# Where the low parts of the attention weights are made, and in which order every engine works: a fused attention and feed-forward kernel

## What is computed

```python
def _L0_attn_ref(x, W_qkv, W_out):
    qkv = x @ W_qkv.T
    q, k, v = jnp.split(qkv, 3, axis=-1)
    ...
    q = phi(q); k = phi(k)                      # elu(x) + 1
    kv_cumsum = jnp.cumsum(k * v, axis=2)
    k_cumsum = jnp.cumsum(k, axis=2)
    out = q * kv_cumsum / (q * k_cumsum + EPS)
    return out @ W_out.T * HD ** (-0.5)

def _L0_ffn_ref(x, w_gate_up, w_proj):
    gu = jnp.einsum('bsd,hd->bsh', x, ternary_quant(w_gate_up))
    gate, up = jnp.split(gu, 2, axis=-1)
    hn = rms_norm(jax.nn.silu(gate) * up)
    return jnp.einsum('bsh,dh->bsd', hn, ternary_quant(w_proj))

x = x + _layernorm(_L0_attn_ref(_layernorm(x), W_qkv, W_out))
x = x + _layernorm(_L0_ffn_ref(_layernorm(x), w_gate_up, w_proj))
```

## Time and profile before

| | |
|---|---|
| runs | 1148.55, 1148.72, 1149.49 us |
| profiled execution | 1149.28 us, of which the span from first to last instruction is 1147.3 us |
| TensorE busy | 1055.8 us, 92% |
| VectorE busy | 805.6 us, 70% |
| GpSimd busy | 561.5 us, 49% |
| ScalarE busy | 487.8 us, 43% |
| mean granted TensorE clock | 0.983 of full |

### The profile page before, as it was taken

The page is one execution under the profiler, slowest core; times in us unless marked ns, Lnnn a source line. Parts: engine busy times, 40 slices in busy tenths (PEclk is TensorE's granted clock), DMA queues, the critical chain, the costliest instruction groups (busy, mean ns, idle before and its releaser), DMA issues.

```text
span 1147.3 us, 14246 instructions
## 1 busy us (share of the span) xinstructions
PE 1055.8 (92%) x5041; PEld 521.7 (45%) x5088; DVE 805.6 (70%) x1233; ACT 487.8 (43%) x808; POOL 561.5 (49%) x494
## 2 busy tenths in 40 slices
PE   3887778988999999999999999999999999999997
PEld 1434344444544454446444454446444454454443
DVE  5899999998557868645884568645884569845424
ACT  4543647664643214542364324542364325423433
POOL 4977548788543534523535234523535244534323
PEclk9998799999999999999999999999999999999999
DMA  7631234410022123003300123003300121001001
GB/s 238 143 97 46 65 101 111 157 56 19 1 74 74 37 74 74 1 8 63 91 24 1 29 83 74 1 10 63 95 18 1 29 83 37 7 32 37 1 1 73
DMA packets 105142, 63.83 MB, mean 56 GB/s; under 512 B 77424, under 2 KB 85616, under 8 KB 105072
## 3 DMA queue, kind: packets, MB, share of 16 engines
q1 hardware_dynamic: 105072, 62.93, 21.1%
HBM read 34.60 MB, written 9.44 MB: 38 GB/s over the span
## 4 chain that ended last, share of the span: by engine, by line
PE 56%; DVE 21%; POOL 6%; issue 6%; ACT 3%; DMA 0%; DVEq 0%; POOLq 0%; ACTq 0%; SPq 0%
PE bank L658 27%; PE bank L693 15%; PE bank L647 6%; PE bank L781 6%; DVE tk L1675 2%; POOL xn L1352 2%; DVE ts L1647 1%; DVE st L1585 1%; DVE grs L1504 1%; DVE hid L1727 1%; DVE x L1771 1%; DVE yq L1540 1%; DVE yq L1554 1%; DVE tr L1657 1%; DVE tq L1621 1%
## 5 line engine op out<-in xcount | busy, mean ns | idle before, releaser
L658 PE MATMUL bank<-x3t,wgu_t 128*128 128x512 f16 x1536 | 347.7, 381 | 15.1 <-DMA x3t<-x3s 8.5
L1363 POOL TENSOR_TENSOR acc<-acc,ht 128x512 f32<-128x512 f32 x90 | 118.3, 1315 | 295.7 <-ACT ht L1055 293.6
L658 PEld LDWEIGHTS bank<-x3t,wgu_t 128*128 128x128 bf16 x1536 | 148.6, 98 | 197.2 <-issue 13.5
L693 PE MATMUL bank<-wproj_t,hid 128*128 128x512 bf16 x830 | 192.8, 379 | 2.7 <-DVE tr L1637 0.5
L1721 DVE TENSOR_TENSOR ht<-ht,bank 128x512 f32<-128x512 f32 x112 | 76.4, 682 | 162.2 <-ACT ht L1016 83.2
L647 PE MATMUL bank<-xnt,wqkv_hi 128*128 128x512 f16 x672 | 163.5, 387 | 13.4 <-issue 10.7
L693 PEld LDWEIGHTS bank<-wproj_t,hid 128*128 128x128 f16 x872 | 84.8, 98 | 101.3 <-DVE tr L1637 1.0
L1727 DVE TENSOR_TENSOR hid<-ht,hid 128x512 f16<-128x512 f32 x109 | 89.5, 821 | 35.1 <-ACT hid L1043 34.0
L1016 ACT ACTIVATE ht<-bank 128x512 f32<-128x512 f32 x112 | 66.4, 593 | 111.2 <-PE bank L658 58.2
L1043 ACT ACTIVATE hid<-ht 128x512 f16<-128x512 f32 x109 | 68.2, 626 | 106.5 <-DVE ht L1721 105.1
L647 PEld LDWEIGHTS bank<-xnt,wqkv_hi 128*128 128x128 f16 x672 | 65.8, 100 | 96.4 <-issue 19.8
(11 more groups left out here) (187 smaller groups left out, 1622.8 us busy)
## 6 DMA issues: line engine op xcount, KB each, us to landing
raw_q<-in_L_ffn_w_gate_up_dram SPq DMA_DIRECT2D x32, 256.0 KB, 2.9
out_dram<-xn SPq DMA_DIRECT2D x7, 1024.0 KB, 8.4
...
```

What stands on the lines that cost most here:

```text
L658: last = pe.matmul(bank[:], wgu_t[:, k, first_row:first_row + P], x3t_of(f)[:, part, k], start=(n == 0), stop=(n == 2 * KD - 1))
L693: last = pe.matmul(bank[:], hid_of(f, part, k)[:, t * P:(t + 1) * P], wproj_t[:, k], start=(k == 0 and part == 0), stop=(k == MT - 1 and p ...
L1363: pool.tensor_tensor(acc[:], acc[:], ht_of(f)[:, m % 2], ALU.add).then_inc(q["acc_done"], 1)
```

## The change

Three things are done. The low parts of tiles 2 and 3 are made on VectorE like those of tiles 0 and 1: `weight_lo` of GpSimd is gone, that of VectorE takes the wait for the buffer, and one semaphore counts all twelve. The lists of all five engines are written anew, in `start()`, `step(s)` and `last_steps()`. No other instruction is added, left out or changed.

```diff
         def wait_low_weights(eng, j, part):
 
-            if j < 2:
-                eng.wait_ge(w_lo, 3 * j + part + 1)
-            else:
-                eng.wait_ge(w_lo_b, 3 * (j - 2) + part + 1)
+            eng.wait_ge(w_lo, 3 * j + part + 1)
...
-            def weight_lo(j, *parts):
-
-                for part in parts:
-                    pool.wait_ge(w_enlarge, powers_for(j))
-                    pool.wait_ge(w_hi, 3 * j + part + 1)
-                    if part == 0:
-                        wait_turned_weights(pool, j - 2)
-                    own_instruction(pool)
-                    pool.tensor_scalar(raw_a[j][:, part], raw_a[j][:, part], enlarge[:, j, part:part + 1], None, ALU.mult).then_inc(w_scaled, 1)
-                    pool.wait_ge(w_scaled, 3 * (j - 2) + part + 1)
-                    pool.tensor_tensor(wsplit[j % 2][:, 1, part], raw_a[j][:, part], wsplit[j % 2][:, 0, part], ALU.subtract).then_inc(w_lo_b, 1)
...
                 for part in parts:
                     dve.wait_ge(w_enlarge, powers_for(j))
                     dve.wait_ge(w_hi, 3 * j + part + 1)
+                    if j >= 2 and part == 0:
+                        wait_turned_weights(dve, j - 2)
                     dve.scalar_tensor_tensor(wsplit[j % 2][:, 1, part], raw_a[j][:, part], enlarge[:, j, part:part + 1],
                                              wsplit[j % 2][:, 0, part], ALU.mult, ALU.subtract).then_inc(w_lo, 1)
```

Of SyncE's list in `start()`, the lines that hold the transposes of the weights:

```diff
-                turn_high_weights(2), load_half(2), turn_x(1, 0, 1), turn_low_weights(2), load_half(0)
-                turn_high_weights(3), turn_x(1, 2, 3), turn_low_weights(3), load_half(3, 4, 5, 7), load_residual(0)
+                turn_high_weights(1), load_raw(4), turn_high_weights(2), turn_x(1, 0), turn_low_weights(2)
+                turn_x(1, 1, 2), load_half(1, 2), turn_high_weights(3), turn_low_weights(3), turn_x(1, 3)
```

More of the change, by code:

```diff
@@ L843, in step @@
+                gate_unit(1, 12), up_unit(1, 12), gate_unit(1, 13), up_unit(1, 13, 14), gate_unit(1, 14, 15)
+                up_unit(1, 15), group(2, 0, 1, 2, 3, 4), square_sums(1), group(2, 5, 6), project(1, 0, 1, 2, 3, 4)
+                group(2, 7), project(1, 5), group(2, 8, 9, 10), project(1, 6), group(2, 11)
+                project(1, 7, 8, 9, 10, 11, 12, 13, 14, 15), group(3, 0, 1), project_att(2, 0, 1, 2, 3), group(3, 2)
             def step(s):
                 f = s - 1
[L845 removed]
@@ new lines, in start @@
+                stats_var("3", 0), sum_keys(1, 2), back_reciprocal(1, 1), carry_key(1, 2), front_products(1, 2)
+                back_output(1, 1), x3_lo(0, 0), scale_sums(5), back_lo(1, 1), x3_lo(0, 1), scale_max(5), clip(2, 3)
+                diff(1), x3_lo(0, 2), feature_q(1, 3), scale_rec(5), x3_lo(0, 3), sum_values(1, 2), round_off(2)
+                feature_k(1, 3), carry_value(1, 2), scale_sums(6), front_products(1, 3), row_shrink(1), diff(2)
+                round_off(3), clip(4), back_reciprocal(1, 2), scale_row(4), scale_max(6), sum_keys(1, 3), diff(3)
@@ new lines, in start @@
+                scale_sums(7), sum_values(1, 3), scale_row(5), carry_key(1, 3), hidden_value(0, 0), scale_bound(2)
+                scale_rec(6), carry_value(1, 3), round_off(4), back_reciprocal(1, 3), back_output(1, 2)
+                hidden_value(0, 1), scale_max(7), back_output(1, 3), back_lo(1, 2), diff(4), back_lo(1, 3)
+                scale_sums(8), clip(5, 6), round_off(5), hidden_lo(0, 0), stats_tile("2", 1, 0), scale_max(8)
+                scale_rec(7), round_off(6), scale_row(6), hidden_lo(0, 1), scale_sums(9), scale_rec(8)
@@ new lines, in start @@
+                hidden_value(0, 2), scale_max(9), diff(5), stats_tile("2", 1, 1, 2), row_shrink(2), hidden_lo(0, 2)
+                stats_tile("2", 1, 3), stats_join("2", 1, 0, 1, 2, 3), scale_row(7), stats_mean("2", 1)
+                stats_var("2", 1), clip(7), diff(6), scale_rec(9), scale_bound(3), clip(8), hidden_value(0, 3)
+                add_ln2_tile(1, 0, 1, 2), stats_tile("3", 1, 0), add_ln2_tile(1, 3), round_off(7), stats_tile("3", 1, 1)
+                scale_sums(10), stats_tile("3", 1, 2), hidden_lo(0, 3), round_off(8), diff(7), stats_tile("3", 1, 3)
@@ new lines, in start @@
+                hidden_value(0, 6), round_off(11), diff(10), scale_max(14), hidden_lo(0, 6), row_shrink(4)
+                scale_rec(13), scale_row(10), scale_sums(15), hidden_value(1, 0), clip(12), scale_rec(14), scale_max(15)
+                diff(11), scale_rec(15), round_off(12), scale_row(11), clip(13), hidden_lo(1, 0), scale_sums(16)
+                scale_bound(5), diff(12), hidden_value(0, 7), round_off(13), scale_sums(17), hidden_lo(0, 7)
+                scale_max(16), hidden_value(1, 1), scale_max(17), clip(14), hidden_value(0, 8), hidden_lo(1, 1)
@@ new lines, in start @@
+                scale_rec(16), diff(13), clip(15), round_off(14), hidden_lo(0, 8), round_off(15), scale_row(12)
+                scale_sums(18), clip(16), diff(14), row_shrink(5), scale_max(18), scale_row(13), scale_rec(17)
+                hidden_value(1, 2), hidden_value(0, 9), scale_bound(6), round_off(16), diff(15), clip(17)
+                hidden_lo(1, 2), stats_tile("1", 2, 0), hidden_value(1, 3), stats_tile("1", 2, 1), scale_rec(18)
+                round_off(17), hidden_lo(0, 9), diff(16), scale_sums(19), hidden_lo(1, 3), row_shrink(6), clip(18)
@@ new lines, in start @@
+                scale_max(19), scale_rec(19), hidden_value(0, 10), scale_sums(20), hidden_lo(0, 10), diff(17)
+                scale_max(20), round_off(18), stats_tile("1", 2, 2), hidden_value(1, 4), scale_sums(21), scale_max(21)
+                scale_rec(20), clip(19), hidden_value(0, 11), clip(20), round_off(19), scale_row(14), diff(18)
+                hidden_lo(1, 4), scale_rec(21), hidden_value(1, 5), diff(19), scale_sums(22), round_off(20)
+                scale_row(15), hidden_value(0, 12), scale_sums(23), scale_max(22), hidden_lo(1, 5), scale_bound(7)
@@ new lines, in start @@
+                diff(20), stats_tile("1", 2, 3), scale_max(23), clip(21), hidden_lo(0, 11), stats_join("1", 2, 0)
+                hidden_lo(0, 12), stats_join("1", 2, 1), scale_rec(22), stats_join("1", 2, 2), row_shrink(7)
+                hidden_value(1, 6), hidden_value(0, 13), scale_rec(23), hidden_lo(1, 6), round_off(21)
+                stats_join("1", 2, 3), hidden_lo(0, 13), stats_mean("1", 2), clip(22), round_off(22), diff(21)
+                hidden_value(1, 7), stats_var("1", 2), clip(23), hidden_value(0, 14), round_off(23), hidden_value(1, 8)
```

646 lines of the change are left out of this document (305 added, 341 removed).

## The result

The changed kernel takes 1118.5 us (median of 4 runs, 1116.7 to 1120.1) against 1149.1 us of the one before in the same session: a ratio of 0.973, 95% interval 0.971 to 0.975. The profiled execution has a span of 1116.2 us against 1147.3 us.

What follows compares the result with a forecast made beforehand. VectorE was taken to bound the start (to 287 us) and TensorE the rest. From 1149.3 us, -5 for the start and -7 for the steps gave 1137.3, less 0.6 to the median: 1136.7 us; range 1127 to 1149.

Steps and rivals of the forecast that it cites:

- one seventh of the 37 us: Start, 29 to 287 us: the new lists save VectorE 5 us of the turns it loses beside GpSimd.
- the four groups: Start: VectorE's diff (9.0 us), clip (13.1), round_off (7.9) and hidden_lo (7.2), whose time above their lone values makes 37 us.
- The start's best case: Second rival: the start gains 16 us, the whole kernel taking 1125.7 us; chance 0.14.
- 7.3 us of waits: Start: TensorE's two early waits for low parts of tiles 2 and 3, 3.59 and 3.69 us, can go.
- The low parts as a draw: Start: on VectorE, 4.4 us of added low-part work against 4 us of turns given back; taken as 0.
- The first rival: The start gains nothing, low parts and their lost turns eating what GpSimd's absence gives: 1141.7 us; chance 0.20.
- The steps: Steady steps: 10 us of TensorE's waits go and 3 us of a new wait come, -7 us in all.
- The 2.8 us of waits for the bank: Steady steps: TensorE's three waits for ScalarE's exp to read the features from a bank, 2.8 us, go.
- The wait at square_sums: Steady steps: a new TensorE wait for GpSimd's squares behind the projection, 0.8 us in each of four steps, 3 us.
- The tail: End of the kernel: the chain of statistics, power and addition per tile is kept; taken as 0.
- The middle: From 287 to 430 us, where TensorE idles 5.4 us: no clear sign, taken as 0 with 2 us either way.
- The third rival: Steps: reciprocal before the last hidden tile comes 3.1 us later than reckoned, steps +5.6 us, 1154.3 us; chance 0.16.

Runs made afterwards that it cites:

- e1: The kernel before with only the low parts of tiles 2 and 3 made on VectorE, other lists as before: 1148.0 us, ratio 0.9985.
- e4: The changed kernel with only the low parts of tiles 2 and 3 put back on GpSimd: 1126.3 us, ratio 0.980.
- e10: The kernel before with GpSimd's divide and scale_back each replaced by three one-input scalings as 128x512 float32, ternary weights not computed rightly: 1221.7 us.
- e3: The changed kernel with last_steps() of all engines as in the kernel before: 1115.3 us, ratio 0.970.

## Why the prediction was wrong

**The step that failed** is "I take one seventh of the 37 us, 5 us, near the low end": the start gave 28.9 us. The mechanism, turns that VectorE loses beside GpSimd's two-input work, was the right one; its size was not, and both factors were too small. The 37 us came from the four groups of the earlier trace rows alone; over all of VectorE's instructions that take turns it is 66.2 us. The features, the running sums, the low parts of x, x3 and the output, and the hidden parts written to hid_b and hid_early (6.0 us) were left out. The features, sums and low parts had more to give than the four kinds: features 8.7 us, sums 6.3, low parts 5.7, against which the low weights and one product lost 3.4 more; 17.3 us net. Diff, clip, round_off and the hidden parts, all three buffers of them, lost 13.9 us less. And the share that can be avoided was 31 of 66 us, nearly half. The reason given, "there are hardly more free places on VectorE than before", counted the reciprocals alone. Reductions, statistics and what reads PSUM take no turns here either: before, 24 reductions took 1.15 to 1.22 us each, 20 statistics 0.63 to 0.69 and 24 `hidden_value` 0.63 to 0.69, whatever GpSimd did. GpSimd's large two-input operations, 165 us to 287 us before and 150 us to 257 us after, lay beside VectorE instructions that take turns for 100 us before and 63 us after, beside reciprocals for 14 and 20, beside the others for 54 and 71.

**The start's best case**, 16 us, had the same fault: "7.3 us of waits and a quarter of the 37". The result lies 13 us beyond it.

**The low parts as a draw** was right by itself: -1.5 us (e1). Its cost was low, since six low parts took 1.08 us in the mean and not 0.73. What it missed is that the move gains value with the lists, 7.8 us (e4): "VectorE bounds the stretch, so this only lets it start earlier" no longer holds once VectorE's turns are gone: without the move it was idle 12.1 us from 40 to 60 us.

**The rule of exclusion.** The first rival rested on the Trainium skill (SBUF — State Buffer, section "Who interferes with whom"), by which a two-input instruction of VectorE contends with any GpSimd instruction that reads SBUF, the port pair that they share being an exclusive lock. For two-input work of GpSimd the rows bear it out: 1.1 us lost in the mean beside scale_back and beside divide. Beside one-input work they do not: in e10, where the scalings lasted 1.49 us, 93 instructions of VectorE that met no other large operation lost 0.15 us in the mean and 0.43 at most. The rival did not come.

**The steps** came out at -6.1 for -7, by other terms. The waits that end from step 4 to step 7 are 7.2 us for x3t before and 3.2 us after, 4.0 us less where 7.2 were reckoned; nearly all that is left, 2.3 us, is the one at step 7, ahead of which the new list has one group less. The 2.8 us of waits for the bank went, as reckoned. The wait at square_sums, put at 3 us, was not there in any step; 2.9 us appeared ahead of project, where nothing had been reckoned. These come to -3.9 us; the rest of the 6.1 us lies in gaps too short to be listed as waits and in TensorE's busy time. **The tail**, put at 0, cost 3 to 4 us (e3): the prediction looked only at its last chain, not at the order in which it begins.

**The middle**, put at 0 with 2 either way: TensorE idles 1.9 us in the 143 us there, for 5.4 before, so some 3.5 us of the gain may lie there. The runs do not separate it from the start; it is within the 28.9 us. The third rival, a late reciprocal, did not come.
